# Layernorm, diagonal recurrence and top-2 experts on one core: expert rows weighted and added by the scatter

## The chip, the cores and the metric

The kernel runs on one core of one Trainium2 chip. The metric is the device time of one execution in microseconds. The five engines of the core are TensorE (PE, with its weight loads as PEld), VectorE (DVE), ScalarE (ACT), GpSimd (POOL) and SyncE (SP, which only issues transfers).

## What is computed

```python
x = L0_attn_x                                   # [8, 1024, 256], 8192 tokens
xn = _layernorm(x, axis=-1)
# s: B_x = xn @ B_w.T + B_b; h_t = sigmoid(log_A) * h_{t-1} + B_x_t; s = h @ C_w.T + C_b
s = _L0_attn_ref(xn, ...)
# experts: 8 of them, the two with the highest logits for each token
logits = xn @ Wr + br
routing_weights, expert_indices = jax.lax.top_k(logits, 2)
routing_weights = jax.nn.softmax(routing_weights, axis=-1)
c = jnp.sum(one_hot(expert_indices, 8) * routing_weights[..., None], axis=-2)
h = silu(xn @ W1[e]) * (xn @ W3[e])             # 256 -> 512
y = h @ W2[e]                                   # 512 -> 256
g = _silu(sum over e of c[e] * y[e])
out = x + s * g
```

All tensors are float32. The tokens are 64 tiles of 128 (`TILES`), in 16 chunks of four tiles (`CHUNKS`, `CT`).

## The kernel before

The kernel is written engine by engine, each with its own program in `build`, and semaphores between them; the order of an engine's instructions is the order of its code.

**Front.** SP loads x chunk by chunk (L260) and stores the normalised rows to `xn_rows` in HBM (L263), 1 KB a token. PE transposes them, computes router logits and the products `bx` (`make_bx`, L973). DVE picks the two experts (L673 to L682), and gives every pair of token and expert a slot, in an order sorted by expert (L698 to L712). Each expert's slots are rounded up to tiles of 256, so there are 71 expert tiles (`EXP_TILES`) with some empty slots. `ratio` = exp(second logit - first) and `weight1` = 1 / (1 + ratio) are kept per token (L456, L716, L717). The table from slots to tokens is made by one-hot matmuls (L726 to L746 on DVE, `invert` on PE), and decoded into `gather_idx` and `scatter_idx` (L747 to L762); an empty slot gets an index beyond the bounds, which the scatter skips.

**Expert tiles.** POOL gathers 2 x 128 rows of `xn_rows` by index for a tile, four tiles ahead (`gather`, L363). PE transposes them (`transpose_x`), forms the gate and the up product, and one tile later the down product (`down`, L1064), each in a high and a low part. ACT copies the low part of y from PSUM (`keep_y_low`, L528), DVE adds the high part (`add_y`, L793) into `y_sb`, a ring of two, and POOL scatters 2 x 128 rows to `y_rows` (`scatter`, L369). `y_rows` has 2 x 8192 rows: one for each token and choice, unweighted. DVE also runs the recurrence (`step_and_scan`) between the first 32 tiles. SP loads the next expert's weights into `raw` when its tiles have been split.

**Tail.** When all has been scattered, SP loads both y rows of a chunk (`load_y`, L284), four chunks ahead (`YY_RING`), and later stores the output (`store_out`, L288). Per chunk: DVE mixes the two rows, `g = ratio * y2 + y1` (`mix`, L873), ACT takes `Silu(weight1 * g)` (`gate_silu`, L580), PE forms the states' product and adds the bias C_b (`states_out`, L1114), DVE multiplies the two (`apply`, L884) and adds x (`add_x`, L893). The states' products of even chunks use PSUM banks 0 and 1, those of odd chunks 2 and 3, so PE may be two chunks ahead of `apply`:

```python
for g in range(CHUNKS):
    if g >= 2:
        eng.wait_ge(u_ready, g - 1)
    states_out(g // 2 * 2, g % 2)
```

The order of POOL through the expert tiles is this loop:

```python
for i in range(EXP_TILES):
    if i + XG_RING < EXP_TILES:
        wait_apart(eng, xT_psum, i + 1)
        gather(i + XG_RING)
    scatter(i)
```

## Time and profile before

| | |
|---|---|
| device time, median of 3 runs | 881.76 us (881.44 to 882.49) |
| device time of the profiled execution | 882.33 us |
| its span, first to last instruction | 880.6 us |
| PE busy | 817.5 us, 93% of the span |
| DVE busy | 521.5 us, 59% |
| ACT busy | 395.5 us, 45% |
| POOL busy | 321.8 us, 37% |
| DMA | 90.78 MB, 103 GB/s mean |

Times in the rows are microseconds from the span's start; idle time and what ended it stand in brackets. In rows by stretch, each engine has its busy time and, in brackets, its instructions; PEclk is the granted clock of TensorE as a share of 2.4 GHz; the share of DMA is that of the 16 DMA engines. A matmul's end is modelled, so rows of PE overlap; the distance from one start to the next is the safer reading. A DMA_INDIRECT row of POOL is the issue of the transfer, not its data's way. A transfer's row in the chain runs from its issue to its landing.

### The profile page before, as it was taken

The numbers are of one execution on the slowest core, as the hardware profiler recorded it, in microseconds if no ns is written. First come the engines' busy times: TensorE is split into PE (matmuls) and PEld (weight loads), VectorE is DVE, ScalarE is ACT, GpSimd is POOL, SyncE is SP. The second block draws the span as 40 slices with busy tenths as digits, with TensorE's granted clock in tenths as the row PEclk, the third lists the DMA queues.
The fourth block names the chain that finished last, engine by engine and source line by source line (L and its number), as shares of the span: only waits on it lengthen the run. The fifth ranks groups of instructions, "written<-read, shape, count | busy, mean of one in ns | idle before, by whom it ended". The sixth has DMA issues, their size and how long they took to land.

```text
span 880.6 us, 17926 instructions
## 1 busy us (share of the span) xinstructions
PE 817.5 (93%) x5608; PEld 731.3 (83%) x5608; DVE 521.5 (59%) x1149; ACT 395.5 (45%) x768; POOL 321.8 (37%) x345
## 2 busy tenths in 40 slices
PE   2579994899999999999999999999999999997996
PEld 2444442899999999999999999999999999995785
DVE  5837896455576665656655444435564644443997
ACT  4564574334453543434545433434444534332442
POOL 3420402244453454444443535344454435321000
PEclk9689997899999999999999999999999999999999
DMA  9952002112131321112232211112332212203997
GB/s 296 313 169 71 1 0 74 58 55 65 49 131 54 101 81 60 60 54 66 96 92 86 93 54 61 58 60 83 100 106 79 62 54 62 57 16 127 360 383 275
DMA packets 65982, 90.78 MB, mean 103 GB/s; under 512 B 7646, under 2 KB 53219, under 8 KB 65956
## 3 DMA queue, kind: packets, MB, share of 16 engines
q1 hardware_dynamic: 51092, 54.80, 18.6%
q0 software_dynamic: 13632, 35.41, 12.8%
q10 hardware_dynamic: 1232, 0.28, 0.2%
q8 instruction: 9, 0.15, 0.1%
q14 instruction: 17, 0.14, 0.1%
HBM read 56.90 MB, written 35.39 MB: 105 GB/s over the span
## 4 chain that ended last, share of the span: by engine, by line
PE 88%; DVE 5%; issue 2%; DMA 2%; ACT 1%; DVEq 0%; SPq 0%; POOL 0%; POOLq 0%; ACTq 0%
PE bank L1046 16%; PE bank L1048 16%; PE bank L1047 16%; PE bank L1076 15%; PE bank L1077 7%; PE bank L1121 6%; PE bank L978 5%; PE bank L1035 3%; DVE stats L609 2%; PE bank L938 2%; PE bank L948 1%; PE bank L1018 1%; PE bank L1117 1%; DMA yy<-y_rows 1%; ACT xnT L401 1%
## 5 line engine op out<-in xcount | busy, mean ns | idle before, releaser
L1046 PE MATMUL bank<-xh,W_sb 128*128 128x256 f32 x1136 | 322.8, 284 | 3.0 <-DVE xl L780 3.0
L1048 PE MATMUL bank<-xl,W_sb 128*128 128x256 f32 x1136 | 322.4, 284 | 0.0
L1047 PE MATMUL bank<-xh,W_sb 128*128 128x256 f32 x1136 | 322.4, 284 | 0.0
L372 POOL DMA_INDIRECT y_rows<-y_sb,scatter_idx x142 | 145.0, 1021 | 326.0 <-DVE y_sb L798 302.7
L786 DVE TENSOR_TENSOR hbuf<-hbuf,bank 128x512 f32<-128x512 f32 x142 | 97.6, 687 | 239.6 <-PE bank L1048 224.8
L1046 PEld LDWEIGHTS bank<-xh,W_sb 128*128 128x128 f32 x1136 | 217.0, 191 | 6.6 <-issue 3.6
L1047 PEld LDWEIGHTS bank<-xh,W_sb 128*128 128x128 f32 x1136 | 217.0, 191 | 0.0
L1048 PEld LDWEIGHTS bank<-xl,W_sb 128*128 128x128 f32 x1136 | 217.0, 191 | 0.0
L1076 PE MATMUL bank<-W_sb,hh 128*128 128x512 f32 x568 | 207.6, 406 | 1.0 <-DVE y_sb L798 1.0
L365 POOL DMA_INDIRECT xg<-xn_rows,gather_idx x142 | 143.3, 1009 | 89.1 <-DVE scatter_idx L762 45.9
L1077 PE MATMUL bank<-W_sb,hl 128*128 128x256 f32 x568 | 158.5, 279 | 0.0
L526 ACT ACTIVATE hh<-hbuf 128x512 fp32r<-128x512 f32 x142 | 89.1, 627 | 108.1 <-DVE hbuf L786 64.5
L522 ACT ACTIVATE hbuf<-bank 128x512 f32<-128x512 f32 x142 | 84.7, 596 | 106.9 <-PE bank L1048 106.7
L1076 PEld LDWEIGHTS bank<-W_sb,hh 128*128 128x128 f32 x568 | 106.8, 188 | 23.3 <-issue 1.2
L1077 PEld LDWEIGHTS bank<-W_sb,hl 128*128 128x128 f32 x568 | 107.3, 189 | 0.0
L530 ACT ACTIVATE y_low<-bank 128x256 f32<-128x256 f32 x142 | 46.8, 381 | 101.4 <-PE bank L1077 99.0
L791 DVE TENSOR_TENSOR hl<-hbuf,hh 128x512 fp32r<-128x512 f32 x142 | 91.9, 684 | 0.1
L780 DVE TENSOR_TENSOR xl<-bank,xh 128x512 fp32r<-128x512 f32 x71 | 49.1, 692 | 36.2 <-ACT xh L516 22.4
L516 ACT ACTIVATE xh<-bank 128x512 fp32r<-128x512 f32 x71 | 42.4, 598 | 52.0 <-PE bank L1035 32.7
L798 DVE TENSOR_TENSOR y_sb<-bank,y_low 128x256 f32<-128x256 f32 x142 | 52.8, 413 | 21.8 <-ACT y_low L530 21.1
L978 PE MATMUL bank<-xnT,BwT 128*128 128x512 f32 (+1 forms) x128 | 62.8, 609 | 1.1 <-issue 1.1
L1121 PE MATMUL bank<-CwT,h_sb 128*128 128x256 f32 x256 | 63.4, 392 | 0.0
(163 smaller groups left out, 720.4 us busy)
## 6 DMA issues: line engine op xcount, KB each, us to landing
yy<-y_rows SPq DMA_DIRECT2D x32, 512.0 KB, 8.1
raw<-L_ffn_W SPq DMA_DIRECT2D x24, 512.0 KB, 3.5
x_sb<-L_attn_x SPq DMA_DIRECT2D x16, 512.0 KB, 9.0
out<-x_sb SPq DMA_DIRECT2D x16, 512.0 KB, 7.6
xn_rows<-h_sb SPq DMA_DIRECT2D x14, 512.0 KB, 5.2
xg<-xn_rows,gather_idx POOLq DMA_INDIRECT x142
y_rows<-y_sb,scatter_idx POOLq DMA_INDIRECT x142
xn_rows<-scratch SPq DMA_DIRECT2D x2, 512.0 KB, 3.0
```

The source lines that it names most:

```text
L365: eng.indirect_dma_start(out=xg[:, i % XG_RING, t, :], out_offset=None, in_=xn_rows, in_offset=bass.IndirectOffsetOnAxis(ap=gather_idx[:, ...
L372: eng.indirect_dma_start(out=y_rows, out_offset=bass.IndirectOffsetOnAxis(ap=scatter_idx[:, 2 * i + t:2 * i + t + 1], axis=0), in_=y_sb[:, ...
L526: eng.activation(hh[:, r, n * 512:(n + 1) * 512], hbuf[:, n * 512:(n + 1) * 512], ACT.Copy).then_inc(hh_ready, 1)
L786: eng.tensor_tensor(half, half, ps_up[n][:, :], ALU.mult).then_inc(h_ready, 1)
L791: eng.tensor_tensor(hl[:, r, cols], hbuf[:, cols], hh[:, r, cols].bitcast(f32), ALU.subtract).then_inc(hl_ready, 1)
L978: last = eng.matmul(bank[2 * q + m][:, :], BwT[:, k, m * P:(m + 1) * P], xnT[:, bass.ds(c, 1), k, :].rearrange("p a c -> p (a c)"), start= ...
L1046: eng.matmul(part, high, x_h, start=k == 0, stop=False)
L1047: eng.matmul(part, low, x_h, start=False, stop=False)
L1048: last = eng.matmul(part, high, x_l, start=False, stop=k == KD - 1)
L1076: eng.matmul(ps_y[t][:, :], h_h, W_sb[:, at:at + 2 * D], start=k == 0, stop=False)
L1077: last = eng.matmul(ps_y[t][:, 0:D], h_l, W_sb[:, at:at + D], start=False, stop=k == KI - 1)
L1121: last = eng.matmul(o, h_g[:, m, t * P:(t + 1) * P], CwT[:, m * D:(m + 1) * D], start=False, stop=t % 2 == 1 and m == KN - 1)
```

## The change

- `y_rows` has one row for each token, and 256 spare rows behind them, as `xn_rows` has. SP writes zeros to `y_rows` and to both spare parts, from a 128 x 256 tile that POOL clears, after the first expert's weights (`zero_rows`). ACT's split of the first weights, whose buffer lies over that tile, and POOL's first gather wait for it.
- Both softmax weights of each token are formed on DVE (`weights`) after the edge one-hots, and stored to `w_rows` in HBM. A second index per slot, `weight_idx`, names the slot's weight. An empty slot now gets a spare row (`token_idx`) instead of an index out of bounds, and one index serves gather and scatter.
- POOL gathers one weight for each slot of a tile (`gather_weights`, 128 rows of 4 bytes each, two transfers a tile), after the scatter of the tile two before.
- ACT's copy of y's low part is scaled by it, and DVE's addition becomes `ps_y * w_slot + y_low`.
- The scatter adds to the row in HBM (`compute_op=ALU.add`), and first waits until the scatter of the tile before has landed.
- Tail: all 16 chunks of y are loaded at once, one row a token, into a buffer for each chunk; `mix` is gone, Silu is one instruction a chunk without scale, and the stores follow. PE's product for chunk c uses one of four pairs of banks (`S_BANKS`), and waits for the product of chunk c - 4, half by half. `add_x` and the last store are in halves.

On POOL, where the program loops over the expert tiles: `xg` is filled by the gather, `w_slot` by the weight gather, `y_rows` by the scatter. Before:

```order
L365 DMA xg<-xn_rows,gather_idx 128x256 [waits xT_psum]
L365 DMA xg<-xn_rows,gather_idx 128x256
L372 DMA y_rows<-y_sb,scatter_idx 16384x256 [waits y_ready]
L372 DMA y_rows<-y_sb,scatter_idx 16384x256
L365 DMA xg<-xn_rows,gather_idx 128x256 [waits xT_psum]
L365 DMA xg<-xn_rows,gather_idx 128x256
```

and with the change:

```order
L372 DMA xg<-xn_rows,token_idx 128x256 [waits xT_psum]
L372 DMA xg<-xn_rows,token_idx 128x256
L387 DMA y_rows<-y_sb,token_idx 8448x256 [waits y_ready,y_stored0]
L387 DMA y_rows<-y_sb,token_idx 8448x256
L378 DMA w_slot<-w_rows,weight_idx 128x1 x2
L372 DMA xg<-xn_rows,token_idx 128x256 [waits xT_psum]
L372 DMA xg<-xn_rows,token_idx 128x256
```

A tile has six transfers where it had four, and the scatter waits for the one before it as well as for DVE.

On PE, at the start of the tail: one row of 512 columns puts the bias into a bank, the next adds half a chunk's products. Before:

```order
L1117 MATMUL bank2<-Cb_rows,pick 128x512
L1121 MATMUL bank2<-CwT,h_sb 128x256 x4
L1117 MATMUL bank3<-Cb_rows,pick 128x512
L1121 MATMUL bank3<-CwT,h_sb 128x256 x4
L1117 MATMUL bank0<-Cb_rows,pick 128x512 [waits u_ready]
L1121 MATMUL bank0<-CwT,h_sb 128x256 x4
```

and with the change:

```order
L1112 MATMUL bank3<-Cb_rows,pick 128x512
L1116 MATMUL bank3<-CwT,h_sb 128x256 x4
L1112 MATMUL bank4<-Cb_rows,pick 128x512 [waits y_ready]
L1116 MATMUL bank4<-CwT,h_sb 128x256 x4
L1112 MATMUL bank6<-Cb_rows,pick 128x512
L1116 MATMUL bank6<-CwT,h_sb 128x256 x4
L1112 MATMUL bank5<-Cb_rows,pick 128x512
L1116 MATMUL bank5<-CwT,h_sb 128x256 x4
L1112 MATMUL bank7<-Cb_rows,pick 128x512
L1116 MATMUL bank7<-CwT,h_sb 128x256 x4
L1112 MATMUL bank0<-Cb_rows,pick 128x512 [waits u_ready]
```

Four halves more stand ahead of the first wait for DVE's product (`u_ready`).

The diff, cut to its core:

```diff
-XG_RING, Y_RING, OH_RING, YY_RING = 4, 2, 8, 4
+XG_RING, Y_RING, OH_RING = 4, 2, 8
+S_BANKS = ((0, 1), (2, 3), (4, 6), (5, 7))
+ZERO_PARTS = 4
...
-    y_rows = nc.dram_tensor("y_rows", [2 * T, D], f32).ap()
+    y_rows = nc.dram_tensor("y_rows", [T + TW, D], f32).ap()
+    w_rows = nc.dram_tensor("w_rows", [P * 2 * TILES, 1], f32).ap()
...
+            w_slot = sb("w_slot", [P, Y_RING, 2], f32, mid)
-            yy = sb("yy", [P, YY_RING, 2, CT, D], f32, tail)
-            g_sb = sb("g_sb", [P, YY_RING, CT, D], f32, tail)
+            yy = sb("yy", [P, CHUNKS, CT * D], f32, tail)
+        zeros = xnT[:, 3, 0, 0:D]
...
         @block.sync
+            def zero_rows():
+                eng.wait_ge(zeros_ready, 1)
+                for n in range(ZERO_PARTS):
+                    j = TILES // ZERO_PARTS
+                    eng.dma_start(y_v[:, n * j:(n + 1) * j, :], zeros.unsqueeze(1).broadcast_to([P, j, D])).then_inc(rows_zeroed, 16)
+                for rows in (xn_rows, y_rows):
+                    eng.dma_start(rows[T:T + TW, :].rearrange("(t p) d -> p t d", p=P), zeros.unsqueeze(1).broadcast_to([P, 2, D])).then_inc(rows_zeroed, 16)
...
+                if e == 0:
+                    zero_rows()
+                    eng.wait_ge(weights_ready, 1)
+                    eng.dma_start(w_rows.rearrange("(p n) a -> p (n a)", p=P), weights[:, :, :].rearrange("p k j -> p (k j)")).then_inc(w_stored, 16)
...
+            for c in range(CHUNKS):
+                eng.dma_start(yy[:, c, :].rearrange("p (t d) -> p t d", t=CT), y_v[:, c * CT:(c + 1) * CT, :]).then_inc(y_loaded[c], 16)
+            for c in range(CHUNKS - 1):
+                eng.wait_ge(out_ready, 2 * c + 2)
+                eng.dma_start(out_v[:, c * CT:(c + 1) * CT, :], x_sb[:, c * CT:(c + 1) * CT, :]).then_inc(out_stored, 16)
...
         @block.gpsimd
+            eng.wait_ge(bx_psum, 2 * 4)
+            eng.memset(zeros, 0.0).then_inc(zeros_ready, 1)
...
+            def gather_weights(i):
+                for t in range(2):
+                    eng.indirect_dma_start(out=w_slot[:, i % Y_RING, t:t + 1], out_offset=None, in_=w_rows,
+                                           in_offset=bass.IndirectOffsetOnAxis(ap=weight_idx[:, 2 * i + t:2 * i + t + 1], axis=0))\
+                       .then_inc(w_loaded[i % Y_RING], 16)
             def scatter(i):
                 wait_apart(eng, y_ready, i + 1)
+                if i:
+                    eng.wait_ge(y_stored[(i - 1) % Y_RING], 32 * ((i - 1) // Y_RING + 1))
                 for t in range(2):
                     eng.indirect_dma_start(out=y_rows,
-                                           out_offset=bass.IndirectOffsetOnAxis(ap=scatter_idx[:, 2 * i + t:2 * i + t + 1], axis=0),
-                                           in_=y_sb[:, i % Y_RING, t, :], in_offset=None, bounds_check=2 * T - 1, oob_is_err=False)\
+                                           out_offset=bass.IndirectOffsetOnAxis(ap=token_idx[:, 2 * i + t:2 * i + t + 1], axis=0),
+                                           in_=y_sb[:, i % Y_RING, t, :], in_offset=None, bounds_check=T + TW - 1, oob_is_err=True,
+                                           compute_op=ALU.add)\
                        .then_inc(y_stored[i % Y_RING], 16)
...
                 scatter(i)
+                if i + Y_RING < EXP_TILES:
+                    gather_weights(i + Y_RING)
...
         @block.scalar
-                    eng.activation(y_low[:, t, :], ps_y[t][:, D:2 * D], ACT.Copy).then_inc(y_low_ready, 1)
+                    eng.activation(y_low[:, t, :], ps_y[t][:, D:2 * D], ACT.Identity, scale=w_slot[:, r, t:t + 1]).then_inc(y_low_ready, 1)
...
+            for c in range(CHUNKS):
+                eng.wait_ge(y_loaded[c], 16)
+                eng.activation(yy[:, c, :], yy[:, c, :], ACT.Silu).then_inc(g_ready, 1)
...
         @block.vector
+            w1, w2 = weights[:, 0, :], weights[:, 1, :]
+            eng.wait_ge(ratio_ready, 1)
+            link(eng.tensor_scalar(w1, w2, 1.0, None, ALU.add))
+            link(eng.reciprocal(w1, w1))
+            eng.tensor_tensor(w2, w2, w1, ALU.mult).then_inc(weights_ready, 1)
...
-                    last = eng.tensor_tensor(y_sb[:, r, t, :], ps_y[t][:, 0:D], y_low[:, t, :], ALU.add)
+                    last = eng.scalar_tensor_tensor(out=y_sb[:, r, t, :], in0=ps_y[t][:, 0:D], scalar=w_slot[:, r, t:t + 1],
+                                                    in1=y_low[:, t, :], op0=ALU.mult, op1=ALU.add)
...
+            def apply(c):
+                eng.wait_ge(g_ready, c + 1)
+                for n, b in enumerate(S_BANKS[c % len(S_BANKS)]):
+                    two = yy[:, c, n * 512:(n + 1) * 512]
+                    eng.wait_ge(s_psum, 2 * c + n + 1)
+                    eng.tensor_tensor(two, two, bank[b][:, :], ALU.mult).then_inc(u_ready, 1)
+            for c in range(CHUNKS):
+                apply(c)
+                if c:
+                    for n in range(2):
+                        add_x(c - 1, n)
+            for n in range(2):
+                add_x(CHUNKS - 1, n)
...
         @block.tensor
+            def states_out(c):
+                h_g = h_half(c // 2 * 2, c % 2)
+                for n, b in enumerate(S_BANKS[c % len(S_BANKS)]):
+                    if c >= len(S_BANKS):
+                        eng.wait_ge(u_ready, 2 * (c - len(S_BANKS)) + n + 1)
+                    eng.matmul(bank[b][:, :], pick[:, :], Cb_rows[:, :], start=True, stop=False)
...
+            for c in range(CHUNKS):
+                if c == 2:
+                    eng.wait_ge(y_ready, EXP_TILES)
+                states_out(c)
```

## Rows read from the trace of the kernel before

**Rows 1.** Busy time by stretch: the front, the one-hot stage, one expert tile
```profile
core 0: us, PE busy (x) PEld busy (x) DVE busy (x) ACT busy (x) POOL busy (x), PEclk, DMA share, GB/s
25.00:50.00 25.00, 15.53 (x92) 10.13 (x92) 14.83 (x72) 17.56 (x37) 9.88 (x8) 0.73 0.80 277
100.00:125.00 25.00, 23.73 (x114) 11.34 (x112) 24.75 (x127) 19.53 (x47) 0.30 (x2) 1.00 0.00 1
397.50:406.40 8.90, 8.90 (x69) 8.55 (x69) 5.05 (x9) 3.55 (x8) 3.79 (x4) 1.00 0.18 59
```

**Rows 2.** Busy time by stretch, the tail
```profile
805.00:820.00 15.00, 9.77 (x35) 7.82 (x34) 7.98 (x17) 5.05 (x12) 0.00 (x0) 0.84 0.97 312
850.00:865.00 15.00, 15.00 (x72) 13.13 (x70) 15.00 (x27) 6.83 (x16) 0.00 (x0) 1.00 1.09 382
```

**Rows 3.** The chain of work that ended last, by engine
```profile
PE 88%; DVE 5%; issue 2%; DMA 2%; ACT 1%; DVEq 0%; SPq 0%; POOL 0%; POOLq 0%; ACTq 0%
```

**Rows 4.** Timeline of PE, start of the tail (start us, us, engine, line, operation)
```profile
801.49 0.47 PE L1117 MATMUL bank<-Cb_rows,pick 128*128 128x512 f32 x1 [2.14 <-DVE Cb_rows L871]
...
806.96 0.59 PE L1117 MATMUL bank<-Cb_rows,pick 128*128 128x512 f32 x1
...
808.93 0.58 PE L1117 MATMUL bank<-Cb_rows,pick 128*128 128x512 f32 x1
...
816.47 0.77 PE L1117 MATMUL bank<-Cb_rows,pick 128*128 128x512 f32 x1 [5.23 <-DVE g_sb L890]
...
820.01 0.58 PE L1117 MATMUL bank<-Cb_rows,pick 128*128 128x512 f32 x1
```

**Rows 5.** Busy time by stretch of 2 us, the granted clock after each idle stretch
```profile
804.00:806.00 2.00, 2.00 (x6) 1.55 (x6) 0.00 (x0) 0.00 (x0) 0.00 (x0) 0.50 0.02 0
...
818.00:820.00 2.00, 2.00 (x7) 1.56 (x6) 2.00 (x4) 1.64 (x4) 0.00 (x0) 0.52 1.10 349
```

**Rows 6.** Timeline of all engines, the last chunks
```profile
867.83 1.67 DVE L879 SCALAR_TENSOR_TENSOR g_sb<-yy,ratio 128x256 f32<-128x256 f32 x4
...
869.63 1.71 ACT L585 ACTIVATE g_sb<-g_sb,weight 128x256 f32<-128x256 f32 x4 [2.21 <-DVE g_sb L879]
...
870.81 0.58 PE L1117 MATMUL bank<-Cb_rows,pick 128*128 128x512 f32 x1
...
873.22 1.28 DVE L890 TENSOR_TENSOR g_sb<-g_sb,bank 128x512 f32<-128x512 f32 x2 [1.39 <-PE bank L1121]
874.42 2.35 DVE L897 TENSOR_TENSOR x_sb<-g_sb,x_sb 128x1024 f32<-128x1024 f32 x2
```

**Rows 7.** The chain in order of time: the last scatter, to its landing
```profile
802.73 2.31 DMA y_rows<-y_sb,scatter_idx
```

**Rows 8.** Timeline of DVE, first instruction on loaded y
```profile
810.52 1.67 DVE L879 SCALAR_TENSOR_TENSOR g_sb<-yy,ratio 128x256 f32<-128x256 f32 x4 [9.18 <-DMA yy<-y_rows]
```

**Rows 9.** The costliest groups: line, shapes, count, busy us, mean ns of one
```profile
L798 DVE TENSOR_TENSOR y_sb<-bank,y_low 128x256 f32<-128x256 f32 x142 | 52.8, 413 | 21.8 <-ACT y_low L530 21.1
```

**Rows 10.** Timeline of POOL: first scatter, one tile, scatter 69 of 0 to 70
```profile
177.75 1.03 POOL L372 DMA_INDIRECT y_rows<-y_sb,scatter_idx  x1 [17.77 <-DVE y_sb L798]
...
411.37 1.02 POOL L372 DMA_INDIRECT y_rows<-y_sb,scatter_idx  x1 [3.81 <-DVE y_sb L798]
...
415.30 0.96 POOL L365 DMA_INDIRECT xg<-xn_rows,gather_idx  x1 [0.30 <-issue]
...
797.03 0.98 POOL L372 DMA_INDIRECT y_rows<-y_sb,scatter_idx  x1 [6.31 <-DVE y_sb L798]
```

**Rows 11.** Timelines of SP, DVE, ACT and POOL in the front
```profile
77.54 79.51 SPq L275 DMA_DIRECT2D raw<-L_ffn_W  x6
...
93.69 0.30 DVE L736 COPY scratch<-bank 128x142 f32<-128x142 f32 x1 [1.08 <-PE bank L1000]
...
140.27 2.93 ACT L490 ACTIVATE W_sb<-raw 128x1024 fp32r<-128x1024 f32 x3
...
146.26 1.94 POOL L365 DMA_INDIRECT xg<-xn_rows,gather_idx  x1 [45.89 <-DVE scatter_idx L762]
```

More of the change, by code:

```diff
@@ L217, in build @@
         tile_done, y_low_ready, y_ready = sem("tile_done"), sem("y_low_ready"), sem("y_ready")
+        w_loaded = [sem(f"w_loaded{q}") for q in range(Y_RING)]
         y_stored = [sem(f"y_stored{q}") for q in range(Y_RING)]
@@ L382, in _ @@
                 gather(i)
+            eng.wait_ge(w_stored, 16)
+            for i in range(Y_RING):
+                gather_weights(i)
             for i in range(EXP_TILES):
@@ L576, in _ @@
             eng.wait_ge(tile_done, EXP_TILES)
[L577 to L591 removed]
+            keep_y_low(last, 0)
+            for c in range(CHUNKS):
+                eng.wait_ge(y_loaded[c], 16)
+                eng.activation(yy[:, c, :], yy[:, c, :], ACT.Silu).then_inc(g_ready, 1)
         @block.vector
@@ L899, in back @@
-            def back(g0, q, by):
-                return (g0, q - by) if q >= by else (g0 - YY_RING, q - by + YY_RING)
-            for q in range(YY_RING):
-                mix(0, q, reused=False)
-                if q >= 1:
-                    apply(0, q - 1)
-                if q >= 2:
-                    add_x(0, q - 2)
-            with loop(eng, YY_RING, CHUNKS, YY_RING) as g0:
-                for q in range(YY_RING):
-                    mix(g0, q)
-                    apply(*back(g0, q, 1))
-                    add_x(*back(g0, q, 2))
@@ L919, in _ @@
+            for c in range(CHUNKS):
[3 more added lines that the diff above has]
+                        add_x(c - 1, n)
+            for n in range(2):
+                add_x(CHUNKS - 1, n)
         @block.tensor
```

126 lines of the change are left out of this document (37 added, 89 removed).

## The prediction

> **What bounds the kernel now.** I read the table by stage first. While the expert tiles run, TensorE (PE) is busy for all of every stretch [rows 1]; the tail also has it full, but there VectorE (DVE) is full too, and the DMA engines stand at 1.09 of their share [rows 2]. The chain gives PE 88% of the way to the end [rows 3]. So what the change can win on DVE and DMA in the tail counts only where PE stands still. The timeline of PE shows where: after the last expert matmul it waits 2.14 us for the bias rows, starts the states' product at 801.49 us, finishes two chunks (four halves, banks 0 to 3) with the half that starts at 808.93, and then stands 5.23 us until DVE frees a bank at 816.47 [rows 4]. Part of its work runs at a low clock: 0.50 at 804 to 806 and 0.52 at 818 to 820, the 1.2 GHz level, each behind one of the two idle stretches [rows 5]. The half that starts at 816.47 takes 3.54 us instead of 1.954. That pitch is (870.81 - 820.01) / 26 halves [rows 4, 6].
>
> Why does DVE come so late? The last scatter leaves at 802.73 and lands 2.31 us later [rows 7]; then y is loaded in pairs, and the first mix starts at 810.52, when two loads have landed [rows 8]. Each chunk costs DVE one mix, one product and one addition, 15.00 us busy in 15 [rows 2], so it cannot catch up: PE and DVE are tied at two halves, 3.91 us, a chunk.
>
> **The tail, step by step.** The mix (four instructions, 1.67 us a chunk [rows 6]) goes, and half of the y loads: 32 loads of 0.52 MB become 16. ScalarE (ACT) applies Silu once to 1024 elements where it had four instructions, 1.71 us [rows 6]. DVE keeps two products (0.64 each: 1.28 for two) and an addition split in halves. I take 0.6 a half, from 1.17 for 1024 (2.35 for two) and 0.64 for 512. That is 2.5 us a chunk against 3.91 of PE [rows 6]. Loads and stores together are now 32 x 0.52 = 16.8 MB; at the tail's 382 GB/s [rows 2] 44 us, against 62.5 us of PE (16 x 3.908). So PE alone bounds the new tail.
>
> PE now writes four chunks before it needs a freed bank. Its four first halves run as before, up to 808.93; the other 28 follow at 1.954, so the last starts at 863.64. DVE took up the last one 2.41 us after its start (870.81 to 873.22) [rows 6]: 866.05 now, instead of 873.22, which is **-7.2 us**. If PE's own pitch is not 1.954 but the 1.97 of the free half from 806.96 to 808.93 [rows 4], the gain is 6.7; if the pitch of before is DVE's, it is a little more. Does chunk 4 find its bank free? It is PE's ninth half and starts at 808.93 + 5 x 1.954 = 818.7. The first chunk of y lands by 810.5 (where two had landed [rows 8]), Silu and one product make it 812.3. That cover is 6.4 us, and it is all that a slower last scatter may cost for nothing.
>
> The end behind PE: before, two products and two additions, 1.28 + 2.35 = 3.6. Now one product and four half additions, because the chunk before stands behind the wait: 0.64 + 2.4 = 3.05, **-0.6**. The last store halves. The old one needed 3.8 us from 876.77 (874.42 + 2.35 [rows 6]) to the span's end at 880.6; 0.26 MB less at 382 GB/s is 0.7, the least is nothing: I take **-0.5**.
>
> **The expert tiles.** Per tile ScalarE's copy of the low part gets a scale, and DVE's addition becomes a scalar_tensor_tensor. The nearest rows: 413 ns for the addition now [rows 9], 1.67 / 4 = 0.42 us for one 128x256 of the new form [rows 6]; ScalarE's copy gets a scale operand, for which I allow 0.1. The y addition is waited for by the next down product, a gate and up product later (the gap in rows 1 is nil), so this is hidden 70 times; it shows once, at the last tile, where PE waits for DVE: **+0.2** (bounds 0 and 0.4).
>
> GpSimd (POOL) is what I looked at longest. One tile of before: two scatters, two gathers, 411.37 to 415.30 + 0.96 = 4.9 us of a tile's (797.03 - 177.75) / 69 = 8.975 [rows 10]. Two weight gathers of 128 rows each come on top. If each costs what a row gather costs, 0.96 + 0.30, that is 2.5, and POOL is at 7.4 of 8.975: 1.5 us left. No row shows a gather of 4 bytes a row or an accumulating scatter. Bounds for one such gather: 0.96 [rows 10], and 1.94, the first one's [rows 11]. For the scatter: 1.02 as now, and 2.04 if issuing it doubles. I take 1.0 and 1.02 to 1.3, because gather and scatter differ by only 0.06 us although one reads HBM by index and the other writes it; then all six are hidden. POOL becomes the bound when a scatter grows by over 0.75 us.
> On this the Trainium skill speaks against the change. Its page "DMA: Bandwidth & Descriptors", section "SWDGE vs HWDGE vs iDMA", says that the cores of GpSimd build one read and one write descriptor for each operation; "Collectives: The Full Stack", section "Stop ④", has the adding DMA read two streams and write one. By that the read side of an accumulating scatter has twice the descriptors, and the sum would be rival (a)'s 909 us, not 873.8. No run here shows it yet.
>
> The scatter of tile i also waits until that of tile i-1 has landed. Before, a scatter landed 2.31 us after its start [rows 7]; the next one starts 8.975 after, the second DMA of the first 1.3 after. Reading and writing back may take up to 7.6 us before this wait shows. DMA share is 0.18 of a tile [rows 1], 1.6 us; it may go to three times that. Hidden.
>
> **The front.** Zeroing writes 8.9 MB from about 83 us (the weight loads ahead of it start at 77.54 [rows 11], and POOL clears its source after the fourth chunk's bx products). At the 277 GB/s at which the front moved data [rows 1], 32 us: done by 116. ScalarE needs it at 140.27, POOL at 146.26 [rows 11], and DMA moved 1 GB/s in between [rows 1]. It would have to fall under 8.9 / 57 = 156 GB/s to be seen. The weights' DVE operations (two before, three now) move behind the edge one-hots, where DVE waits 1.08 us for PE anyway [rows 11]. In the index chain one linked operation goes and two unlinked come, 0.2 to 0.3 each: **+0.1** (bounds -0.1, +0.4). POOL's four weight gathers ahead of its loop take 5 us; scatter 0 waits 17.8 us there [rows 10]. Nothing.
>
> **Sum.** -7.2 - 0.6 - 0.5 + 0.2 + 0.1 = -8.0 on a profiled execution of 882.33 us (span 880.6): 874.3. The median of the runs shown lies 0.57 below that execution, so the forecast is 873.8 us. Adding the bounds gives 872.5 to 875.5.
>
> **Rivals.** (a) POOL becomes the bound, through the issue of the accumulating scatter. At 2.04 each a tile costs it 4.9 + 2.5 + 2.0 = 9.5 against 8.975, in 69 tiles: +35 us, 909 us. Against it: gather and scatter now cost nearly the same [rows 10]. For it: an add must read its destination as well, which no row prices. The page's rule above would make this the outcome. It decides from 1.77 us an issue on. 13%. This is the one that ends slower; milder forms (1.8, or a dearer weight gather) end at 875 to 890.
> (b) The add is slow in the DMA engines: a pair lands later than 7.6 us after its start, POOL waits for it, then DVE for y_sb. At 9 us a tile becomes 10.3: +90 us, 964. From the point on each 0.1 us costs 7 us. 4%. If it lands in 5 to 7 us, the last one still fits the 6.4 us of cover.
> (c) The early chunks don't help, because the loads hold each other up: the DMA share was 1.09 there [rows 2]. If 16 loads in flight share the bandwidth evenly, all land together at 805 + 8.4 MB / 0.382 = 827; then PE waits for its fifth chunk until 829, 10 us, and the result is 883. Against: with eight in flight the first pair landed by 810.5 [rows 8], after 5 us, not after 11. 5%.
> (d) The states' clock: PE no longer stops at 816, so the second low stretch goes. That is in the sum. Should PE stay at the low level for four more halves, +5 us: 879. 3%.
>
> **How the numbers follow.** The forecast with its bounds has 75%. The range from 871.5 to 884 holds it, (c), (d) and the mildest part of (a); it leaves (b) and most of (a) out, and some 3% below. Faster by over 0.2% (1.8 us, about what a measurement of this kernel can tell from no change) has the forecast, (d) and the mild (a): 80%. Same 5%, slower 15%.
>
> **What would show it.** PE in the tail: 32 halves from about 801.8 with one low-clock stretch and no idle; last DVE addition ends near 869.5, span near 872.6. POOL: six DMA_INDIRECT a tile of 0.95 to 1.3 us, idle ahead of the scatter still released by DVE's y_sb, pitch 8.975. Wrong would be a releaser "DMA y_rows" ahead of the scatter, PE gaps ahead of the down product, or the first Silu later than 817.

## The result, and the profile after

The changed kernel takes 930.05 us, median of 4 runs (925.84 to 934.67), where the one before took 882.12 in the same session: 1.0541 times the time, 95% interval 1.0515 to 1.0568. It is 48 us slower; the forecast was 873.8. The profiled execution took 928.71 us (span 926.8).

The page of the changed kernel, lines of its parts 1, 3, 4 and 5 (part 5: busy us, mean ns of one, idle us before and what ended most of it):

```profile
PE 832.7 (90%) x5608; PEld 737.5 (80%) x5608; DVE 505.9 (55%) x1103; ACT 395.0 (43%) x720; POOL 572.0 (62%) x489
...
q0 software_dynamic: 31808, 37.32, 24.9%
...
PE 83%; DVE 8%; issue 3%; another core or an unknown queue 3%; ACT 1%; DVEq 1%; DMA 1%; ACTq 0%
...
L387 POOL DMA_INDIRECT y_rows<-y_sb,token_idx x142 | 228.8, 1611 | 92.8 <-DVE y_sb L813 45.1
...
L1069 PE MATMUL bank<-W_sb,hh 128*128 128x512 f32 x568 | 213.5, 415 | 32.2 <-DVE hbuf L801 27.6
...
L372 POOL DMA_INDIRECT xg<-xn_rows,token_idx x142 | 149.1, 1050 | 88.2 <-DVE weight_idx L777 45.2
L378 POOL DMA_INDIRECT w_slot<-w_rows,weight_idx x142 | 159.6, 1124 | 43.3 <-issue 43.3
...
L813 DVE SCALAR_TENSOR_TENSOR y_sb<-bank,w_slot,y_low 128x256 f32<-128x256 f32 x142 | 61.4, 474 | 36.7 <-ACT y_low L554 24.7
```

PE has fallen from 88% of the chain [rows 3] to 83%, and "another core or an unknown queue" is new in it, on one core. The queue of POOL's transfers (q0) is at 24.9% of the DMA engines' time, before 12.8% of a shorter span. Issuing a scatter costs POOL 1.61 us, a weight gather 1.12. PE stands 32 us ahead of the down product, where it had no gap in a tile [rows 1].

POOL in the expert stage, timeline of the changed kernel: the first scatter, one tile, and the end:

```profile
182.46 1.64 POOL L387 DMA_INDIRECT y_rows<-y_sb,token_idx  x1 [17.61 <-DVE y_sb L813]
...
407.58 1.61 POOL L387 DMA_INDIRECT y_rows<-y_sb,token_idx  x1 [0.30 <-issue]
409.50 1.57 POOL L387 DMA_INDIRECT y_rows<-y_sb,token_idx  x1 [0.30 <-issue]
411.38 1.03 POOL L378 DMA_INDIRECT w_slot<-w_rows,weight_idx  x1 [0.30 <-issue]
412.71 0.99 POOL L378 DMA_INDIRECT w_slot<-w_rows,weight_idx  x1 [0.31 <-issue]
414.00 0.94 POOL L372 DMA_INDIRECT xg<-xn_rows,token_idx  x1 [0.30 <-issue]
415.25 0.95 POOL L372 DMA_INDIRECT xg<-xn_rows,token_idx  x1 [0.30 <-issue]
416.50 1.62 POOL L387 DMA_INDIRECT y_rows<-y_sb,token_idx  x1 [0.30 <-issue]
...
852.61 1.61 POOL L387 DMA_INDIRECT y_rows<-y_sb,token_idx  x1 [1.53 <-DVE y_sb L813]
854.53 1.57 POOL L387 DMA_INDIRECT y_rows<-y_sb,token_idx  x1 [0.30 <-issue]
859.08 1.55 POOL L387 DMA_INDIRECT y_rows<-y_sb,token_idx  x1 [2.99 <-DMA y_rows<-y_sb,token_idx]
```

Before, the same scatter waited 3.81 us for DVE [rows 10]; now POOL issues without a pause. From tile 0 to tile 69 a tile takes (852.61 - 182.46) / 69 = 9.71 us, before 8.975 [rows 10]: +50.9 us in 69 tiles. The first scatter is 4.7 us later (182.46, before 177.75), and the tail gives back 9.5 (below). With 0.1 between the last scatters and the tail that is the 46.2 us by which the spans differ.

But POOL is not all of it. Of POOL's waits, this view of the changed kernel (total, times, longest) leaves 45.1 - 17.6 = 27.5 us in 15 scatters for which POOL did wait for DVE:

```profile
POOL y_rows L387 <- DVE y_sb L813: 45.1, 16, 17.6
POOL y_rows L387 <- issue: 44.7, 125, 3.1
```

And one such stretch, in the timeline of the changed kernel:

```profile
414.52 0.28 PE L1041 MATMUL bank<-xl,W_sb 128*128 128x256 f32 x1
...
417.20 0.60 ACT L545 ACTIVATE hbuf<-bank 128x512 f32<-128x512 f32 x1 [3.13 <-remote]
...
419.45 0.69 DVE L801 TENSOR_TENSOR hbuf<-hbuf,bank 128x512 f32<-128x512 f32 x1 [4.72 <-remote]
...
420.20 0.50 PE L1069 MATMUL bank<-W_sb,hh 128*128 128x512 f32 x1 [2.08 <-DVE hbuf L801]
```

The second half of the gate product is over at 414.80 (414.52 + 0.28), and ACT, idle for 3.13 us, starts its Silu at 417.20. Besides this result the Silu waits only for DVE to be done with its buffer, and DVE was. The view says "remote" because PE's record had ended long before the wait did. (A matmul's end is modelled, so the trace does not tell whether the product itself or only the news of it came late.) I call this a **late result** and count it with one measure: how long after both the end of the half's last matmul and its own previous instruction ACT starts the Silu, by the trace, from 200 to 790 us. It leaves out lateness that falls while ACT is busy, so it is a lower bound. Before it is 0.03 us on the mean and never over 0.10. In the changed kernel 40 of 121 are over 0.5 us and the longest is 3.53. This was no rival of mine.

### The profile page after: what moved, and what is told of

It is laid out like the page before. It is cut to its first block, busy times and chain, and to the rows that moved or that the text cites. A ratio compares the mean times of both kernels' runs of the same rounds, so it can differ in the third digit from the quotient of the medians.

```text
span 926.8 us, 17796 instructions
## 1 busy us (share of the span) xinstructions
PE 832.7 (90%) x5608; PEld 737.5 (80%) x5608; DVE 505.9 (55%) x1103; ACT 395.0 (43%) x720; POOL 572.0 (62%) x489
## 3 DMA queue, kind: packets, MB, share of 16 engines
q0 software_dynamic: 31808, 37.32, 24.9%
## 4 chain that ended last, share of the span: by engine, by line
PE 83%; DVE 8%; issue 3%; another core or an unknown queue 3%; ACT 1%; DVEq 1%; DMA 1%; ACTq 0%
PE bank L1041 16%; PE bank L1069 15%; PE bank L1039 14%; PE bank L1040 14%; PE bank L1070 7%; PE bank L1116 6%; PE bank L971 5%; DVE hbuf L801 2%; PE bank L931 2%; PE bank L1028 2%; DVE stats L624 1%; PE bank L941 1%; PE bank L1112 1%; PE bank L1011 1%
## 5 line engine op out<-in xcount | busy, mean ns | idle before, releaser
L387 POOL DMA_INDIRECT y_rows<-y_sb,token_idx x142 | 228.8, 1611 | 92.8 <-DVE y_sb L813 45.1
L1069 PE MATMUL bank<-W_sb,hh 128*128 128x512 f32 x568 | 213.5, 415 | 32.2 <-DVE hbuf L801 27.6
L372 POOL DMA_INDIRECT xg<-xn_rows,token_idx x142 | 149.1, 1050 | 88.2 <-DVE weight_idx L777 45.2
L378 POOL DMA_INDIRECT w_slot<-w_rows,weight_idx x142 | 159.6, 1124 | 43.3 <-issue 43.3
L1070 PE MATMUL bank<-W_sb,hl 128*128 128x256 f32 x568 | 161.3, 284 | 0.0
L554 ACT ACTIVATE y_low<-bank,w_slot 128x256 f32<-128x256 f32 x142 | 59.5, 470 | 111.8 <-PE bank L1070 76.0
L813 DVE SCALAR_TENSOR_TENSOR y_sb<-bank,w_slot,y_low 128x256 f32<-128x256 f32 x142 | 61.4, 474 | 36.7 <-ACT y_low L554 24.7
L1116 PE MATMUL bank<-CwT,h_sb 128*128 128x256 f32 x256 | 60.4, 379 | 0.0
```

The costliest lines, as they stand in the source:

```text
L372: eng.indirect_dma_start(out=xg[:, i % XG_RING, t, :], out_offset=None, in_=xn_rows, in_offset=bass.IndirectOffsetOnAxis(ap=token_idx[:, 2 ...
L378: eng.indirect_dma_start(out=w_slot[:, i % Y_RING, t:t + 1], out_offset=None, in_=w_rows, in_offset=bass.IndirectOffsetOnAxis(ap=weight_id ...
L387: eng.indirect_dma_start(out=y_rows, out_offset=bass.IndirectOffsetOnAxis(ap=token_idx[:, 2 * i + t:2 * i + t + 1], axis=0), in_=y_sb[:, i ...
L1069: eng.matmul(ps_y[t][:, :], h_h, W_sb[:, at:at + 2 * D], start=k == 0, stop=False)
L1070: last = eng.matmul(ps_y[t][:, 0:D], h_l, W_sb[:, at:at + D], start=False, stop=k == KI - 1)
L1116: last = eng.matmul(o, h_g[:, m, t * P:(t + 1) * P], CwT[:, m * D:(m + 1) * D], start=False, stop=t % 2 == 1 and m == KN - 1)
```

## The experiments

Theory A: POOL is the bound by what it issues (2 x 1.61 + 2 x 1.05 + 2 x 1.12 + 6 x 0.31 = 9.4 us a tile, over PE's 8.9). Theory B: the landing. Theory C: the added transfers disturb PE.

**The scatter plain again.**
```diff
-                                           in_=y_sb[:, i % Y_RING, t, :], in_offset=None, bounds_check=T + TW - 1, oob_is_err=True,
-                                           compute_op=ALU.add)\
+                                           in_=y_sb[:, i % Y_RING, t, :], in_offset=None, bounds_check=T + TW - 1, oob_is_err=True)\
```


> The changed kernel with the scatter plain again (rows are overwritten, so the two expert rows of a token are not summed); the weight gathers, the waits and the tail stay. Theory A (POOL is the bound by what it issues): the scatter's issue falls from 1.61 to about 1.02 us, POOL's sum per tile from about 9.43 to 8.25 us on the mean, under PE's 8.91; the pitch from scatter to scatter returns from 9.67 to about 8.9, the stage ends some 50 us earlier: 872 to 880 us. Theory B (the landing of the accumulating scatter, some 4.5 us, is waited for before the next scatter): also about 875, since a plain one lands in 2.3. Theory C (the 4-byte gathers themselves disturb the others): stays above 900.

Measured: 1057.53 us, with a wide spread (1038.59 to 1066.56), 175 us over before (156 to 184). The numbers of A and B are wrong by far; C's "above 900" holds. POOL's issue did fall (1040 ns a scatter), POOL is 46% busy and waits for DVE 264 us; yet the tile takes longer. The end of the first half of the gate product, the weight loads of PE in the up product behind it, and ACT's Silus, in this kernel's timeline:

```profile
275.27 0.28 PE L1040 MATMUL bank<-xl,W_sb 128*128 128x256 f32 x1
...
278.15 0.19 PEld L1038 LDWEIGHTS bank<-xh,W_sb 128*128 128x128 f32 x1
278.27 0.19 PEld L1039 LDWEIGHTS bank<-xh,W_sb 128*128 128x128 f32 x1
279.22 0.19 PEld L1040 LDWEIGHTS bank<-xl,W_sb 128*128 128x128 f32 x1 [0.76 <-issue]
279.94 0.19 PEld L1038 LDWEIGHTS bank<-xh,W_sb 128*128 128x128 f32 x1 [0.53 <-issue]
280.63 0.19 PEld L1039 LDWEIGHTS bank<-xh,W_sb 128*128 128x128 f32 x1 [0.51 <-issue]
...
282.09 0.60 ACT L544 ACTIVATE hbuf<-bank 128x512 f32<-128x512 f32 x1 [5.91 <-remote]
...
287.08 0.60 ACT L544 ACTIVATE hbuf<-bank 128x512 f32<-128x512 f32 x1 [4.39 <-remote]
```

Inside the up product, with no wait in the program, PE's instructions come 0.7 us apart instead of 0.12. The gate half that is over at 275.55 by PE's record (275.27 + 0.28) reaches ACT at 282.09, 5.9 us after ACT was free for it. This lies in a run of twelve indirect DMAs that POOL issues without a pause, from 269.95 to 285.22. The chain on its page:

```profile
PE 62%; another core or an unknown queue 16%; DVE 8%; issue 6%; DVEq 3%; ACT 2%; ACTq 1%; DMA 0%
```

**No weight gathers in the loop.**
```diff
-                if i + Y_RING < EXP_TILES:
-                    gather_weights(i + Y_RING)
...
-                eng.wait_ge(w_loaded[r], i * 16 + (32 - 16 * r))
+                eng.wait_ge(w_loaded[r], 32)
```


> The changed kernel with the weights gathered for the first two tiles alone (later tiles take those weights, so the weighting is left out); scatters stay accumulating. Theory A: POOL issues 2 x 1.61 + 2 x 1.05 + 4 x 0.3 = 6.5 us per tile, the pitch returns to about 8.9 and the time to 872 to 880. Theory B: the wait for the landing is still there, pitch about 9.6, 925 to 932. Theory C as the accumulating transfers (24.9% of the DMA engines' time) disturbing PE's results: also above 900, and the late arrivals behind gate and up products (mean 0.50 us) stay.

Measured: 877.78 us, 0.9943 of before (0.9922 to 0.9965), inside A's range; no late result over 0.04 us. Its scatters still take POOL 1.62 us each, and its tiles take 8.98 us, as before. So four DMAs a tile with the accumulating scatter, issue and landing, cost nothing. B falls, and with it C where it meant the accumulating transfers.

**The weights travel with the row.** A version with the whole computation:
```diff
-    xn_rows = nc.dram_tensor("xn_rows", [T + TW, D], f32).ap()
+    xn_rows = nc.dram_tensor("xn_rows", [T + TW, D + 2], f32).ap()
...
+            def pick_w(i, q):
+                for t in range(2):
+                    last = eng.scalar_tensor_tensor(out=w_slot[:, bass.ds(2 * i + t, 1)], in0=xg[:, q, t, D + 1:D + 2],
+                                                    scalar=choice2[:, bass.ds(2 * i + t, 1)], in1=xg[:, q, t, D:D + 1],
+                                                    op0=ALU.mult, op1=ALU.add)
+                last.then_inc(w_picked, 1)
...
-                    wait_apart(eng, xT_psum, i + 1)
+                    wait_apart(eng, w_picked, i + 1)
```


> A version with the whole computation: each row of xn_rows carries the token's first weight and the difference to its second in two more columns, so the x gather brings them, and DVE picks the slot's weight in two operations on one column each. Four indirect DMAs a tile instead of six; scatters accumulate. Theory A: POOL about 6.5 us per tile, PE bounds again, and the tail's gain of 9.5 us shows: 870 to 878 us, faster than both. Theories B and C: above 900. If the 1032-byte rows cost PE or the gathers something, a few us more.

Measured: **867.59 us, 0.9830 of before (0.9811 to 0.9849)**. It beats both kernels, and is 2.4 us under the range expected. Its page has PE's chain share at 90%, and POOL waits for DVE again:

```profile
PE 90%; DVE 5%; ACT 1%; issue 1%; DMA 1%; DVEq 0%; POOL 0%; ACTq 0%
...
L381 POOL DMA_INDIRECT y_rows<-y_sb,token_idx x142 | 230.2, 1621 | 220.9 <-DVE y_sb L809 190.2
```

The scatter costs the same 1.62 us as in the changed kernel. Of 14.0 us that the span is shorter than before, 9.5 are the tail (69.6 us from PE's first half to the end, before 79.1). The tiles give most of the rest: 8.90 us each, before 8.975. No run tells why they are a little shorter.

**The tail two chunks deep**, in that version:
```diff
-S_BANKS = ((0, 1), (2, 3), (4, 6), (5, 7))
+S_BANKS = ((0, 1), (2, 3))
```


> The version with the weights in the row, with the state products of the tail two chunks deep instead of four (bank pairs (0,1) and (2,3) alone). By the forecast's step on the tail, PE is then held from chunk 2 on until DVE has multiplied chunk 0: 5 to 9 us slower than four deep. If the late loads alone set the tail, less than 2 us.

Measured: 875.76 us, 8.2 more by the medians; from PE's first half to the span's end 76.6 us against 69.6, so 7.0. The idle stretch of [rows 4] is back in its timeline of PE:

```profile
801.91 0.58 PE L1111 MATMUL bank<-Cb_rows,pick 128*128 128x512 f32 x1
809.58 0.76 PE L1111 MATMUL bank<-Cb_rows,pick 128*128 128x512 f32 x1 [5.37 <-DVE yy L894]
```

Next: what about the weight gathers does the harm? Theory D: their 4 bytes a row. Theory E: six indirect DMAs one behind the other. The next three add a function behind the scatters, `more(i)`, whose target nothing reads (left out for the last three tiles; the 4-byte form views xn_rows as rows of one element, and waits on the target are not shown):

```diff
+            def more(i):
+                for t in range(2):
+                    eng.indirect_dma_start(out=extra[:, i % 2, t, :], out_offset=None, in_=xn_rows,
+                                           in_offset=bass.IndirectOffsetOnAxis(ap=token_idx[:, 2 * i + t:2 * i + t + 1], axis=0))\
+                       .then_inc(extra_done[i % 2], 16)
...
                 scatter(i)
+                if i < EXP_TILES - 3:
+                    more(i)
```


> The version with the weights in the row, and two more row gathers of 1032 bytes a row for each tile behind its scatters, into a tile that nothing reads: six indirect DMAs a tile again, no 4-byte ones. Theory D (it is the 4-byte gathers that hold up PE's results): POOL 9.1 to 9.4 us a tile, no late PE results, time between 875 and 905 us by POOL's issue alone. Theory E (it is six indirect DMAs a tile back to back, whatever their size): about as the changed kernel, 920 to 935 us or more, PE's results up to 3 us late.

> The same, but the two added gathers bring 4 bytes a row. Both theories expect the changed kernel's time, 920 to 935 us, and PE's results late, though nothing waits for what these gathers bring; 868 to 880 would say that it was the wait for the weights, not the gathers.

> The kernel before with two 4-byte gathers a tile added behind its plain scatters, into a tile that nothing reads. POOL issues 6 x 1.0 + 6 x 0.3 = 7.8 us a tile, under PE's 8.9. Theory A (issue time alone): no change, 882 us. Theories D and E: as the changed kernel with plain scatters, slower by 50 to 180 us, with PE's results late by several us.

For the last, two POOL operations take the DMAs' place:
```diff
+                for t in range(2):
+                    link(eng.tensor_scalar(extra[:, 0, t, :], x_sb[:, t, :], 2.0, None, ALU.mult))
```


> The version with the weights in the row, and two POOL operations on 128 x 256 (about 1.28 us each) for each tile behind its scatters instead of DMAs, into a tile that nothing reads. POOL is as busy as with six indirect DMAs, 9.1 us a tile. Theory E as POOL being busy without a pause: 900 us or more and late PE results. Theories D, and E as the issuing of DMAs: 868 to 890 us, no PE result late.

Measured: 929.09, 932.60, 1070.74 and 891.45 us. Rows of 1032 bytes do as much harm as 4 bytes, so D falls, and nothing has to wait for them. The kernel before, with plain scatters and two small gathers more, loses 188 us, though POOL's own time is 7.9 us a tile, and A as a full explanation falls with it. Part of the 188 us may be TensorE's clock: it is 0.90 on the mean of that execution, where the kernel before has 0.97, and PE is busy for 889 us in place of 818. In that kernel's timeline of POOL, 10.78 us of waiting stand behind a run of DMAs without a pause:

```profile
429.45 0.94 POOL L367 DMA_INDIRECT xg<-xn_rows,gather_idx  x1 [0.30 <-issue]
430.70 0.95 POOL L367 DMA_INDIRECT xg<-xn_rows,gather_idx  x1 [0.30 <-issue]
442.42 1.02 POOL L382 DMA_INDIRECT y_rows<-y_sb,scatter_idx  x1 [10.78 <-DVE y_sb L813]
```

With arithmetic instead of DMAs the mean pitch from scatter to scatter is 9.28 us, set in the main by POOL's own work and its waits for it, and the longest late result 0.76 us: 24 us over the version without it. With two row gathers in their place POOL's own work, its longer waits taken off, is 9.28 us a tile as well. So the 38 us from there to 929.09 belong to indirect DMAs as such.

Then doses and pauses, in the kernel before: one gather instead of two (`for t in range(1)`); two of 16 rows; one operation between scatters and added gathers; a wait in its place.

> The kernel before with one 4-byte gather a tile added, five indirect DMAs instead of six: POOL issues 6.5 us a tile and pauses some 2.4. Theory E (PE's results are held up while indirect DMAs follow one another without a pause): 882 to 890 us, hardly a late result; if it is the mean number per microsecond with no threshold between four and six, about half of the 188 us.

```diff
-                    eng.indirect_dma_start(out=extra[:, i % 2, t, :], out_offset=None, in_=xn_rows.rearrange("t (d a) -> (t d) a", a=1),
-                                           in_offset=bass.IndirectOffsetOnAxis(ap=gather_idx[:, 2 * i + t:2 * i + t + 1], axis=0))\
+                    eng.indirect_dma_start(out=extra[0:16, i % 2, t, :], out_offset=None, in_=xn_rows.rearrange("t (d a) -> (t d) a", a=1),
+                                           in_offset=bass.IndirectOffsetOnAxis(ap=gather_idx[0:16, 2 * i + t:2 * i + t + 1], axis=0))\
```


> The kernel before with two 4-byte gathers of 16 rows a tile added instead of 128 rows. If what counts is the number of rows (descriptors), 882 to 890 us; if it is the number of instructions, 1000 us or more. POOL's issue time of 16 rows against 128 shows what of its 1.0 us goes by the row.

```diff
+                    link(eng.tensor_scalar(pause[:, :], x_sb[:, 0, :], 2.0, None, ALU.mult))
                     more(i)
```


> The kernel before with two 4-byte gathers of 128 rows and one POOL operation on 128 x 256 (about 1.3 us) between the scatters and those gathers. More work on POOL, 9.1 to 9.4 us a tile, over PE's 8.9. Theory E: the pause in the issuing lets the results through, so this is faster than the same without it (1071 us), 890 to 960 us. Any theory in which POOL's load alone counts: 1071 us or more.

```diff
+                    eng.wait_ge(y_stored[i % Y_RING], 32 * (i // Y_RING + 1))
                     more(i)
```


> The same as the last, but instead of the operation POOL waits until the two scatters have landed (some 2.3 us) before it issues the added gathers. A tile then takes POOL 10 us: theory E gives 950 to 980 us with few late results, less than the 1071 us without the wait; a load theory gives more than 1071.

Measured: 882.52, 882.01, 882.50 and 912.00 us, none with a result later than 0.10 us. Five DMAs a tile are free. Two of 16 rows are too, though issuing one still takes 0.89 us of the 0.99 that 128 rows take: POOL's time has hardly changed, the loss of 188 us is gone. Nor do packets decide: POOL's queue moves 17984 of them with 16 rows as with 128. And more work on POOL cures it. The timeline of POOL with the pause:

```profile
413.70 1.02 POOL L383 DMA_INDIRECT y_rows<-y_sb,scatter_idx  x1 [0.30 <-issue]
415.03 1.00 POOL L383 DMA_INDIRECT y_rows<-y_sb,scatter_idx  x1 [0.30 <-issue]
416.04 0.92 POOL L403 TENSOR_SCALAR pause<-x_sb 128x256 f32<-128x256 f32 x1
417.23 1.38 POOL L376 DMA_INDIRECT extra<-xn_rows,gather_idx  x1 [0.28 <-POOL pause L403]
...
421.41 0.95 POOL L368 DMA_INDIRECT xg<-xn_rows,gather_idx  x1 [0.30 <-issue]
422.66 1.02 POOL L383 DMA_INDIRECT y_rows<-y_sb,scatter_idx  x1 [0.30 <-issue]
```

POOL is full, 422.66 - 413.70 = 8.96 us a tile, and the kernel is as fast as before. With the wait for the landing (1.71 us a tile in its timeline) POOL is over PE's pitch, and that costs 30 us, but 159 less than without the wait.

Does the pause cure the changed kernel? Three runs on it with an operation between scatters and weight gathers (128 x 256, or a memset of one column), and the short one in the kernel before:

```diff
                 scatter(i)
                 if i + Y_RING < EXP_TILES:
+                    link(eng.tensor_scalar(pause[:, :], x_sb[:, 0, :], 2.0, None, ALU.mult))
                     gather_weights(i + Y_RING)
```


> The changed kernel with one POOL operation on 128 x 256 (0.92 us at the least) between the scatters and the weight gathers. POOL's sum per tile is then 9.9 us at the least and 10.3 on the mean of its durations so far. If results held up are most of the loss: they vanish, and the time is at or under the 930 us. If POOL's sum is what costs: pitch 9.9 to 10.3 us, 940 to 975 us, with no late result.

> The changed kernel with the scatter plain (the two rows of a token are not summed) and the same pause. POOL's sum 8.8 to 9.1 us a tile. Theory E: no late results, 872 to 885 us against 1057 without the pause.

```diff
-                    link(eng.tensor_scalar(pause[:, :], x_sb[:, 0, :], 2.0, None, ALU.mult))
+                    link(eng.memset(pause[:, :], 0.0))
```


> The kernel before with the two 4-byte gathers, and a pause that is a memset of one column (about 0.1 us, and the wait for it) instead of the 0.9 us operation. If any other instruction between the DMAs is enough: 882 us. If the length of the pause decides: between 882 and 1071, near the latter.

> The changed kernel with that memset of one column between scatters and weight gathers; POOL's sum grows by 0.2 to 0.4 us a tile, 14 to 28 us over all tiles. If the short pause lets PE's results through: 915 to 950 us with no late result, the whole loss being POOL's sum. If it does nothing: 945 to 960 us with late results.

Measured: 965.02, 950.35, 1069.81 and 927.32 us. In the first, POOL waits for DVE nowhere between the first scatter and the last tiles, the mean pitch of 10.2 us is the sum of what it does, and that is the whole loss; there are still late results (33 of 116 over 0.5 us), against what I expected, but nobody waits for them, since all wait for POOL. The second recovers some 107 of 175 us (two sessions, and the 175 has the spread told above), not all, against what I expected: 49 of 117 results over 0.5 us late, up to 4.4 us. In the third a pause of 0.13 us does nothing: up to 8.9 us late. In the last it does not let the results through either (53 of 121 over 0.5 us late, up to 4.3), though the time is in the band where I expected none late. The memset there is free, because it runs while the accumulating scatter's issue ends: 0.66 us from 406.69 where the scatter's record goes on to 407.24:

```profile
405.67 1.57 POOL L388 DMA_INDIRECT y_rows<-y_sb,token_idx  x1 [0.30 <-issue]
406.69 0.66 POOL L410 MEMSET pause<- 128x1 f32 x1
407.62 1.03 POOL L379 DMA_INDIRECT w_slot<-w_rows,weight_idx  x1 [0.27 <-POOL pause L410]
```

The last two, on the version with the weights in the row: `more(i)` with one gather of 1032 bytes a row, and the last chunk stored whole.

> The version with the weights in the row and one more row gather of 1032 bytes a row a tile, five indirect DMAs, two of them accumulating: POOL's sum about 8.1 us a tile, with short pauses before the scatters. If the loss needs POOL at or over PE's 8.9 us: 866 to 870 us, no late result. If it sets in earlier: over 875.

```diff
-            for c in range(CHUNKS - 1):
+            for c in range(CHUNKS):
...
-            for n in range(2):
-                at = (CHUNKS - 1) * CT + n * CT // 2
-                eng.wait_ge(out_ready, 2 * CHUNKS - 1 + n)
-                eng.dma_start(out_v[:, at:at + CT // 2, :], x_sb[:, at:at + CT // 2, :]).then_inc(out_stored, 16)
```


> The version with the weights in the row, with the last chunk stored in one piece instead of two. The forecast put the halving at 0.5 us: 868 us, within what the measurement can tell; over 1.5 us more would say that it was under-sized.

Measured: 868.62 us (867.94 to 869.14) and 868.39 us (867.21 to 870.30). Five DMAs fit also with two of them accumulating; five Silus in 132 come over 0.5 us late, up to 1.12. The whole store costs nothing: both spans end 69.6 us after PE's first half.

Every run on one page; POOL's DMAs a tile stand with the scatters first:

| run | indirect DMAs a tile | late over 0.5 us, longest | us |
|---|---|---|---|
| before | 2 plain + 2 | none, 0.10 | 882 |
| before, one more | 2 + 3 | none, 0.10 | 882.5 |
| before, two more of 16 rows | 2 + 4 | none, 0.10 | 882.0 |
| before, two more and 0.9 us pause | 2 + 4 | none, 0.10 | 882.5 |
| before, two more and wait for landing | 2 + 4 | none, 0.04 | 912.0 |
| before, two more and 0.13 us pause | 2 + 4 | 34 of 100, 8.9 | 1069.8 |
| before, two more | 2 + 4 | 30 of 101, 7.2 | 1070.7 |
| weights in the row | 2 adding + 2 | none, 0.10 | 867.6 |
| the same, one more | 2 adding + 3 | 5 of 132, 1.1 | 868.6 |
| the same, two more of 4 bytes | 2 adding + 4 | 35 of 119, 3.8 | 932.6 |
| the same, two more | 2 adding + 4 | 40 of 120, 3.9 | 929.1 |
| the same, arithmetic | 2 adding + 2 | 11 of 128, 0.76 | 891.5 |
| changed | 2 adding + 4 | 40 of 121, 3.5 | 930.1 |
| changed, no weight gathers | 2 adding + 2 | none, 0.04 | 877.8 |
| changed, pause | 2 adding + 4 | 33 of 116, 3.1 | 965.0 |
| changed, short pause | 2 adding + 4 | 53 of 121, 4.3 | 927.3 |
| changed, scatter plain, pause | 2 plain + 4 | 49 of 117, 4.4 | 950.4 |
| changed, scatter plain | 2 plain + 4 | 32 of 100, 5.9 | 1057.5 |

## Why the prediction was wrong

**POOL's step failed**: "then all six are hidden. POOL becomes the bound when a scatter grows by over 0.75 us". The scatter grew by 0.59 (1.61 against 1.02), and POOL was the bound all the same. The step has two faults. The first is sizes: by its own terms POOL had 4.9 + 2.5 = 7.4 us a tile, and with 2 x 0.59 that would be 8.6, still under 8.975; everything at its mean gives 9.4. Some 0.3 of the difference was missing before any change: the 4.9 runs from one scatter's start to the last gather's end and holds three of the four pauses of 0.30 that a tile has. For the rest it took the best tile for the mean: the tile above takes 416.50 - 407.58 = 8.92 us without a pause, but gathers of 1.3 to 2.0 us lie in many tiles, and the mean of the weight gather was 1.12 and not the 1.0 taken.

The second is a mechanism that the step doesn't have: that indirect DMAs from POOL cost only POOL's time. The kernel before with two small gathers more had 7.9 us of POOL in a tile, the very picture of that step, and lost 188 us. In the changed kernel both act. Of 50.9 us in 69 tiles, the 27.5 us that POOL waited for DVE are late results, and the other 23 are POOL's own sum. One of the forecast's own signs of being wrong, PE gaps ahead of the down product, came with them. The split is a reading of one trace and not shown by a run; the runs bracket it: arithmetic in place of two DMAs costs 24 us, the two DMAs 62.

**The rule weighed against it** was right in its sign. Reading two streams and writing one, as the Trainium skill has it in "Collectives: The Full Stack", section "Stop ④", would by my reckoning have doubled the issue, to 2.04 us and 909 us. The trace shows 1.61, and the adding scatters use more of the DMA engines: q0 is at 24.9% of 926.8 us and moves 31808 packets, against 11.2% of 1050.9 us and 18176 packets with them plain. But the versions without weight gathers keep the 1.62 us and are faster than before. So rival (a) had the sign and the engine; the price of the scatter counts only on top of six DMAs a tile. What the plain scatter does is the reverse of its rule: cheaper to issue, and over 100 us slower. That six DMAs then follow one another faster is the likely reason, not a shown one. (The rival's own sum is a little high: 4.89 + 2.52 + 2.04 = 9.45, which is 33 us and 907.)

**The landing**: the pair at 852.61 lands at 859.08, when the next may start; counted from its second DMA 4.55 us, before 2.31 [rows 7], inside the "up to 7.6 us". POOL waits for it only at the end, where the last tiles come closer together. Rival (b) is out.

**The front** was right but for one sentence. Zeroing was over long before 140 us, the first gather came at 145.91 (146.26 before), in place of +0.1. The sentence "POOL's four weight gathers ahead of its loop take 5 us; scatter 0 waits 17.8 us there. Nothing." failed, by 4.7 us. Fourteen DMAs follow one another there without a pause, before ten. The second half of PE's up product of tile 0 is over at 163.68 by PE's record, and DVE, free since 164.26, starts on it at 166.48; before, DVE stood 0.76 us at this place. The timeline of the changed kernel:

```profile
163.40 0.28 PE L1041 MATMUL bank<-xl,W_sb 128*128 128x256 f32 x1
...
166.48 0.69 DVE L801 TENSOR_TENSOR hbuf<-hbuf,bank 128x512 f32<-128x512 f32 x1 [2.22 <-remote]
```

PE then stands 3.81 us and comes back at the lower clock once more. Both kernels by stretch, before first:

```profile
150.00:175.00 25.00, 18.93 (x124) 17.99 (x125) 8.35 (x13) 7.76 (x12) 7.84 (x8) 0.78 0.29 93
```
```profile
150.00:175.00 25.00, 16.76 (x92) 16.18 (x93) 5.01 (x7) 6.13 (x9) 11.50 (x12) 0.65 0.29 91
```

A granted clock of 0.65 against 0.78 means more of the stretch at the 1.2 GHz level. Without those four gathers (weights in the row) the first scatter is at 178.02. The other five kernels that have them start it between 180.6 and 184.6 us, the other ones without them between 176.2 and 179.5.

**The tail** was right, and a little small. Predicted -8.3 with the end behind PE; measured -9.5. The timeline of the changed kernel:

```profile
857.21 0.47 PE L1112 MATMUL bank<-Cb_rows,pick 128*128 128x512 f32 x1 [2.35 <-DVE Cb_rows L887]
...
868.65 1.06 ACT L606 ACTIVATE yy<-yy 128x1024 f32<-128x1024 f32 x1 [12.91 <-DMA yy<-y_rows]
...
917.66 0.58 PE L1112 MATMUL bank<-Cb_rows,pick 128*128 128x512 f32 x1
...
920.61 2.49 DVE L901 TENSOR_TENSOR x_sb<-yy,x_sb 128x512 f32<-128x512 f32 x4
922.53 1.37 SPq L312 DMA_DIRECT2D out<-x_sb  x2
```

32 halves without a gap, as the step "PE now writes four chunks" had it. First to last start is 60.45 us, before 69.32: -8.9 where the step had -7.2. Four chunks deep alone is worth 7.0 by the run two deep. Another 1.7 is a sentence of the sum, "Its four first halves run as before": they took 1.85 to 1.96 each here, since no low clock came behind the 2.35 us of waiting (the granted clock stays 1.00 from 850 to 870 us, where before it fell to 0.50 [rows 5]). The version with the weights in the row has the same; no run tells why. The end behind PE is 926.8 - 917.66 = 9.1 us, before 9.8: the -0.6 holds, the -0.5 for the halved store is nothing. Rivals (c) and (d) are out: the first Silu is 11.4 us behind PE's first half and PE's fifth chunk finds its bank free.

The sign thus came from the expert tiles (+50.9 us) and, for a small part, the front (+4.7). What the forecast described, with POOL's step true, is the version with the weights in the row: 867.6 us against 873.8.

**Not settled**: why PE's results, and with plain scatters its instructions too, come late while POOL issues indirect DMAs almost without a pause. Shown are conditions. A fifth DMA of 128 rows a tile costs nothing, a sixth brings the loss, two more of 16 rows don't. It comes with 4 bytes a row and with 1032, with plain and with adding scatters, and POOL busy with arithmetic instead leaves little of it. In the kernel before with two gathers more, 0.9 us of other work between the DMAs takes it away whole, and a wait there takes the late results away. In the changed kernel such a pause leaves the late results there, and with plain scatters gives back a part of the time; why was not tried further.

## What to carry to other kernels

Count indirect DMAs a tile, not only POOL's time for them: here, in tiles of 9 us, a fifth of 128 rows was free and a sixth cost 60 to 190 us. A small value that belongs to a row travels best with the row. When a consumer is idle while the profile calls its releaser "remote" on one core, compare its start with the end of the record it waits for, and look at what the DMA issuer is doing without a pause.

## What the runs showed of the hardware that was not expected

- ACT, free for it, waited for a finished PE result up to 3.5 us in the changed kernel, and up to 7.2 us in the kernel before with two gathers more (8.9 with the short pause); with four or five indirect DMAs a tile and plain scatters, at most 0.10.
- In those stretches with plain scatters PE's own instructions came 0.7 us apart instead of 0.12.
- A cheaper instruction (the plain scatter, 1.04 us against 1.61) made a kernel over 100 us slower, and a 0.9 us operation without any use made one 188 us faster.
- A gather of 16 rows costs POOL 0.89 us, one of 128 rows 0.99: nearly all of it is by the instruction. The memset behind an adding scatter on POOL started 0.55 us before the scatter's record ended, in the rows above; DMAs start 0.30 us after it.
- An adding scatter moves more packets than a plain one: POOL's queue has 31808 against 18176 in the same kernel, 96 more for each of 142 scatters.
